# Cross-attention and a routed feed-forward on one core: GpSimd's instructions in another order, new first slots, kept rows as a full tile

## The reference, cut to what matters

```python
def xattn(input, feats):            # 16 heads of 16 features
    q = heads(input @ Wq + bq)
    k, v = heads(feats @ Wkv + bkv)
    scores = einsum('bhqd,bhkd->bhqk', q, k) / sqrt(D)
    attn = softmax(scores, axis=2)  # over the queries, not the keys
    return merge(einsum('bhqk,bhkd->bhqd', attn, v)) @ Wo + bo

def ffn(x):                         # 96 of 128 tokens of a batch
    scores = einsum('bld,d->bl', x, w_router)
    _, top_idx = top_k(scores, 96)
    processed = gelu(x[top_idx] @ w_block)       # tanh form
    return x.at[top_idx].set(processed)

x = x + xattn(layernorm(x), ctx_1024)
x = x + ffn(layernorm(x))
```

## Time and profile before

| what | value |
|---|---|
| time, median of 3 runs | 902.03 us (901.85 to 904.2) |
| the profiled execution's own time | 903.28 us |
| span, first to last instruction | 901.5 us |
| busy, share of the span: PE / PEld / DVE / ACT / POOL | 96% / 84% / 95% / 97% / 88% |
| granted TensorE clock, mean | 0.992 of full speed |
| DMA, share of 16 engines | 26% in queue 1, under 1% in the others |

### The profile page before, as it was taken

One profiled execution on the slowest core, in us unless ns is written; L12 is line 12 of the kernel. 1 busy time (PEld: TensorE's weight loads), 2 busy tenths in 40 slices (PEclk: granted clock), 3 DMA queues, 4 the chain that ended last, 5 costly groups with the idle time before them and its releaser, 6 DMA issues. The chain is left out here.

```text
span 901.5 us, 31626 instructions
## 1 busy us (share of the span) xinstructions
PE 868.3 (96%) x10562; PEld 755.4 (84%) x10562; DVE 854.4 (95%) x2068; ACT 872.5 (97%) x4632; POOL 795.0 (88%) x1487
## 2 busy tenths in 40 slices
PE   7899999999999999999999999999999999999972
PEld 6688888888888888888888888888888888888852
DVE  6889999999999999999999999999999999999987
ACT  5899999999999999999999999999999999999984
POOL 4568889999999999999999999999999999998865
PEclk9999999999999999999999999999999999999996
DMA  6221223233233223223223233223222222312102
GB/s 202 61 68 51 65 67 93 59 87 93 59 88 96 59 86 95 59 87 94 69 78 92 60 89 91 76 71 91 79 73 88 82 70 86 96 43 55 49 25 93
DMA packets 70978, 70.48 MB, mean 78 GB/s; under 512 B 12064, under 2 KB 62752, under 8 KB 70816
## 3 DMA queue, kind: packets, MB, share of 16 engines
q1 hardware_dynamic: 69456, 67.68, 26.2%
q10 hardware_dynamic: 1360, 0.79, 0.3%
HBM read 35.13 MB, written 16.78 MB: 58 GB/s over the span
## 5 line engine op out<-in xcount | busy, mean ns | idle before, releaser
L593 ACT ACTIVATE e_sb<-ps_s,neg_max 128x128 f32<-128x128 f32 x2048 | 770.0, 607 | 3.6 <-DVE neg_max L751 3.3
L593 ACT ACTIVATION_READ_ACCUMULATOR e_sb<-ps_s,neg_max 128x1 f32 x2048 | 704.0, 431 | 0.0
L751 DVE TENSOR_REDUCE neg_max<-ps_s 128x4 f32<-128x512 f32 x512 | 331.8, 668 | 25.8 <-PE ps_s L349 24.4
L349 PE MATMUL ps_s<-q_eo,k_sb 32*128 32x256 f32 x2048 | 146.6, 400 | 2.3 <-DVE recip L804 1.4
L414 PE MATMUL ps_a<-e_sb,v_pad 128*32 128x128 f32 x4096 | 138.4, 276 | 2.1 <-POOL v_pad L1085 0.9
L310 PE MATMUL ps_a<-w_o_sb,o_sb 128*128 128x256 f32 x512 | 133.2, 383 | 3.2 <-DVE v_sb L858 3.0
L414 PEld LDWEIGHTS ps_a<-e_sb,v_pad 128*32 128x32 f32 x4096 | 104.1, 109 | 23.7 <-issue 21.3
L349 PEld LDWEIGHTS ps_s<-q_eo,k_sb 32*128 32x128 f32 x2048 | 94.0, 184 | 30.8 <-issue 26.0
L1085 POOL TENSOR_TENSOR v_pad<-v_sb,recip 128x256 f32<-128x256 f32 x128 | 79.7, 623 | 31.8 <-DVE recip L811 29.8
L1074 POOL TENSOR_TENSOR x_sb<-x_sb,bo_sb 128x256 f32<-128x256 f32 x128 | 106.2, 831 | 0.2
L303 PE MATMUL ps_t<-w_z_hi,xt_hi 128*128 128x258 f32 x256 | 96.4, 376 | 2.2 <-DVE z_sb L870 2.2
(11 more groups left out here) (109 smaller groups left out, 2465.5 us busy)
## 6 DMA issues: line engine op xcount, KB each, us to landing
x_sb<-in_x SPq DMA_DIRECT2D x64, 256.0 KB, 2.9
c_sb<-in_ctx SPq DMA_DIRECT2D x64, 256.0 KB, 3.1
out<-z_sb SPq DMA_DIRECT2D x64, 256.0 KB, 2.4
q_eo<-q_raw SPq DMA_DIRECT2D x504, 32.0 KB, 2.0
z_sb<-in_L_xattn_Wkv ACTq DMA_DIRECT2D x2, 256.0 KB, 7.4
z_sb<-in_L_xattn_Wq ACTq DMA_DIRECT2D x1, 256.0 KB, 4.2
w_z_sb<-in_L_ffn_w_block SPq DMA_DIRECT2D x1, 256.0 KB, 7.7
w_o_sb<-in_L_xattn_Wo SPq DMA_DIRECT2D x1, 256.0 KB, 7.0
```

What stands on the lines that cost most here:

```text
L349: mm = nc.tensor.matmul(ps_s[:, bank(b, j), c, :, :], k_sb[rows, r2, c, h * T:(h + 1) * T], q_eo[rows, r2, :, c, h, :], start=True, stop=True)
L593: last = nc.scalar.activation(e_sb[:, b % 4, j, c, par, :], ps_s[:, bank(b, j), c, par, :], ACT.Exp, bias=neg_max[:, b % 4, h:h + 1], accu ...
L751: nc.vector.tensor_reduce(neg_max[:, b % 4, :].rearrange("p (c j q) -> p j c q", c=C, j=J)[:, j, :, :], ps_s[:, bank(b, j), :, :, :], AX.X ...
```

## The change

Four things change, and none of the arithmetic.

1. GpSimd's loop is reordered so that instructions with scalars and with two tensors alternate; `rstd1_of_pair` and `rstd2_of_pair` are split into a variance and a root, the values stand between them, input and bias directly behind the unprocessed row, and `gelu_square` always has its wait.
2. `gelu_product` works on batch s-8 in place of s-7, with the last one behind the loop.
3. The first slots of TensorE, ScalarE and VectorE have another order.
4. `keep_row` has 128 rows in place of 8, cleared once by a memset; its transpose is a full 128x128 one, of which VectorE reads the first 8 columns.

```diff
--- before.py
+++ after.py
@@ -98,7 +98,7 @@
         recip = sb("recip", [P, 4, H])
         cand = sb("cand", [GROUP, T])
         top8 = sb("top8", [GROUP, 8])
-        keep_row = sb("keep_row", [GROUP, T])
+        keep_row = sb("keep_row", [P, T])
         half_keep = sb("half_keep", [P, 2, GROUP])
         drop_rstd = sb("drop_rstd", [P, 2, GROUP])
         alpha = sb("alpha", [P, 2, GROUP])
@@ -125,7 +125,7 @@
         ps_xt = ps_q[:, 0:E]
         ps_z = ps_t[:, 0:ZW]
         ps_fifth = ps_s[:, J, :, :, :].rearrange("p c q t -> p (c q t)")
-        ps_cand, ps_keep, ps_mean = ps_fifth[0:GROUP, 0:T], ps_fifth[:, T:T + GROUP], ps_a[:, 0:ZW]
+        ps_cand, ps_keep, ps_mean = ps_fifth[0:GROUP, 0:T], ps_fifth[:, T:2 * T], ps_a[:, 0:ZW]
 
         def bank(b, j):
             return J if j == 0 and b % 2 == 1 else j
@@ -499,7 +499,7 @@
                 if b % GROUP == 0 and has(b):
                     pe.wait_ge(keep_row_ready, upto(b + 7))
                     pe.wait_ge(exp_ready[0], upto(b + 15))
-                    nc.tensor.transpose(ps_keep, keep_row[:, :], ident[0:GROUP, 0:GROUP]).then_inc(keep_mm, 8)
+                    nc.tensor.transpose(ps_keep, keep_row[:, :], ident[:, :]).then_inc(keep_mm, 8)
 
             transpose_inputs(0)
             transpose_inputs(1)
@@ -512,9 +512,9 @@
             queries_or_keys(2, 0)
             transpose_inputs(4)
             queries_or_keys(2, 1)
+            scores(1)
             mean_of_block_weights()
             transpose_inputs(5)
-            scores(1)
             values(0)
             transpose_inputs(6)
             queries_or_keys(4, 0)
@@ -666,8 +666,8 @@
             inputs_high(4)
             exps(0, 1)
             exps(0, 0)
+            exps(1, 3)
             inputs_high(5)
-            exps(1, 3)
             exps(1, 2)
             inputs_high(6)
             exps(1, 1)
@@ -898,13 +898,13 @@
                     dve.wait_ge(top_dropped, b + 8)
                     if has(b - 1):
                         dve.wait_ge(keep_mm, b)
-                    nc.vector.tensor_scalar(keep_row[:, ::-1], cand[:, :], LOWEST, None, ALU.is_gt).then_inc(keep_row_ready, 8)
+                    nc.vector.tensor_scalar(keep_row[0:GROUP, ::-1], cand[:, :], LOWEST, None, ALU.is_gt).then_inc(keep_row_ready, 8)
                 elif step == 10:
                     dve.wait_ge(keep_mm, b + 8)
                     dve.wait_ge(rstd2_ready, b + 8)
                     g, r = (b // GROUP) % 2, b % R
-                    nc.vector.scalar_tensor_tensor(drop_rstd[:, g, :], ps_keep, -1.0, rstd2[:, r:r + GROUP], ALU.add, ALU.mult)
-                    nc.vector.tensor_scalar(half_keep[:, g, :], ps_keep, 0.5, None, ALU.mult).then_inc(keep_col_ready, 8)
+                    nc.vector.scalar_tensor_tensor(drop_rstd[:, g, :], ps_keep[:, 0:GROUP], -1.0, rstd2[:, r:r + GROUP], ALU.add, ALU.mult)
+                    nc.vector.tensor_scalar(half_keep[:, g, :], ps_keep[:, 0:GROUP], 0.5, None, ALU.mult).then_inc(keep_col_ready, 8)
 
             def final(b, settled=False):
 
@@ -938,24 +938,24 @@
             inputs_low(3)
             for j in (3, 2, 1, 0):
                 maxima(0, j)
+            queries(2)
             weights_low("v")
-            queries(2)
             inputs_low(4)
+            inverse_sums_23(0)
+            keys(2)
             stats1_of_pair(6)
-            keys(2)
-            centre_block_weights()
-            inverse_sums_23(0)
             maxima(1, 3)
             maxima(1, 2)
+            centre_block_weights()
+            inverse_sums_01(0)
+            maxima(1, 1)
             inputs_low(5)
-            inverse_sums_01(0)
             values_and_bias(0)
-            maxima(1, 1)
             maxima(1, 0)
             inputs_low(6)
+            inverse_sums_23(1)
             stats1_of_pair(8)
             queries(4)
-            inverse_sums_23(1)
 
             for s in range(2, B):
                 sure = 20 <= s < B - 1
@@ -1037,20 +1037,26 @@
         @block.gpsimd
         def _(pool):
             nc.gpsimd.memset(ident[:, :], 0.0).then_inc(mask_step, 1)
+            nc.gpsimd.memset(keep_row[:, :], 0.0).then_inc(mask_step, 1)
             nc.gpsimd.memset(minus_half[:, :], -0.5).then_inc(mask_step, 1)
             nc.gpsimd.memset(w_z_sb[:, :, E + 1:E + 2], 0.0).then_inc(mask_step, 1)
             nc.gpsimd.memset(minus_mean[:, :], -1.0 / E).then_inc(mask_step, 1)
-            pool.wait_ge(mask_step, 4)
+            pool.wait_ge(mask_step, 5)
             nc.gpsimd.affine_select(out=ident[:, :], in_=ident[:, :], compare_op=ALU.not_equal, fill=1.0, base=0,
                                     pattern=[[-1, P]], channel_multiplier=1).then_inc(const_ready, 1)
             nc.gpsimd.memset(q_eo[:, 1, :, :, :, :], 0.0).then_inc(q_eo_zero, 1)
 
-            def rstd1_of_pair(b):
+            def variance1_of_pair(b):
 
                 if b % 2 == 0 and has(b):
                     r = slice(b % R, b % R + 2)
                     pool.wait_ge(st1_ready, upto(b + 1))
                     nc.gpsimd.tensor_scalar(ve1[:, r], m2_1[:, r], 1.0 / E, EPS, ALU.mult, ALU.add).then_inc(ve1_ready, 2)
+
+            def root1_of_pair(b):
+
+                if b % 2 == 0 and has(b):
+                    r = slice(b % R, b % R + 2)
                     nc.gpsimd.tensor_scalar(neg_m1[:, r], mean1[:, r], -1.0, None, ALU.mult)
                     pool.wait_ge(ve1_ready, upto(b + 1))
                     nc.gpsimd.tensor_tensor(rstd1[:, r], ve1[:, r], minus_half[:, :], ALU.pow).then_inc(rstd1_ready, 2)
@@ -1088,12 +1094,22 @@
                                             .to_broadcast([P, H // 2, 2, D]),
                                             ALU.mult).then_inc(v_pad_ready, 1)
 
-            def rstd2_of_pair(b):
+            def rstd1_of_pair(b):
+
+                variance1_of_pair(b)
+                root1_of_pair(b)
+
+            def variance2_of_pair(b):
 
                 if b % 2 == 0 and has(b):
                     r = slice(b % R, b % R + 2)
                     pool.wait_ge(st2_ready, upto(b + 1))
                     nc.gpsimd.tensor_scalar(ve2[:, r], m2_2[:, r], 1.0 / E, EPS, ALU.mult, ALU.add).then_inc(ve2_ready, 2)
+
+            def root2_of_pair(b):
+
+                if b % 2 == 0 and has(b):
+                    r = slice(b % R, b % R + 2)
                     pool.wait_ge(ve2_ready, upto(b + 1))
                     nc.gpsimd.tensor_tensor(rstd2[:, r], ve2[:, r], minus_half[:, :], ALU.pow).then_inc(rstd2_ready, 2)
 
@@ -1194,19 +1210,23 @@
             for s in range(4, B):
                 sure = 20 <= s < B - 1
                 normalise(s + 7, sure)
-                rstd1_of_pair(s + 9)
-                rstd2_of_pair(s - 4)
-                gelu_square(s - 5, sure)
+                gelu_square(s - 5)
+                variance1_of_pair(s + 9)
+                variance2_of_pair(s - 4)
                 values_over_sums(s - 1, sure)
+                root1_of_pair(s + 9)
+                root2_of_pair(s - 4)
                 scale_and_shift(s - 16)
                 unprocessed(s - 16, sure)
+                input_and_bias(s + 4)
                 gelu_factor(s - 5)
+                gelu_product(s - 8)
                 gelu_sum(s - 7)
-                input_and_bias(s + 4)
                 gelu_cubic(s - 5)
-                gelu_product(s - 7)
-
-            rstd2_of_pair(B - 4)
+
+            gelu_product(B - 8)
+            variance2_of_pair(B - 4)
+            root2_of_pair(B - 4)
             gelu_factor(B - 5)
             scale_and_shift(B - 16)
             values_over_sums(B - 1)
```

## The result

The changed kernel took **915.12 us** (median; 914.87 to 916.16) beside 901.94 us (901.66 to 904.2) for the kernel before: a ratio of 1.0145, 95% interval [1.0133, 1.0157]. It is slower by 13 us, where 899.3 us was forecast. Two executions among those of the experiments (970.84 and 1210.61 us, at granted clocks of 0.85 and 0.65 in the mean) are left out of all medians and ratios. The profiled execution took 915.23 us (span 913.4).

| stretch | before | after | difference |
|---|---|---|---|
| to score matmul 16 | 124.20 | 122.47 | -1.73 |
| 13 groups of 8 steps, each | 53.63 | 54.72 | +1.09, in all +14.17 |
| score matmul 120 to 127 | 45.84 | 45.00 | -0.84 |
| score matmul 127 to the end | 34.3 | 34.6 | +0.3 |

The account below looks back on a forecast made before the run. It took ScalarE's casts to bound the main loop, 53.52 us a group, TensorE's group being 0.12 us above. Terms -1.2 (loop), -1.3 (start) and -0.2 (rest) sum to -2.7 us: 902.03 to 899.3 us, range 897.6 to 902.4.

Parts of the forecast that it names:

- What the order moves: Main loop: GpSimd's new order makes its input-and-bias sum delay VectorE's final sum, 0.24 us a group against 0.10 before.
- rival 2: Main loop: GpSimd wins the port in steps without second norm and with kept rows; 54.06 us a group, 906.0 us; chance 0.10.
- The alternation: GpSimd's loop: each broken-up pair gives 0.12 us, some 0.4 us a step, costed at nothing because GpSimd waits for reciprocals anyway.
- Kept rows: TensorE's full-tile transpose, one step in eight: 0.13 us in place of 0.35; with collisions, main loop gains 1.2 us.
- ScalarE's floor: Main loop: ScalarE's casts, 6.69 us apart, allow no group of eight steps under 53.52 us.
- First slots: Kernel start: reordered lists start score matmuls 1 and 2 near 22.0 and 29.85 us, gaining 1.3 us.
- The rest: Memset, later gelu product and last steps: net -0.2 us, mostly from fewer final-sum stalls at the end.

Follow-up runs that it names:

- The three kernels with late sums in some steps: Changed kernel, sum of input and bias moved behind the gelu sum only in steps 0; 5, 6, 7; or 1 to 7: 912.59, 904.48, 902.02 us.
- the late sum: Changed kernel with only GpSimd's sum of input and bias moved back behind the gelu sum, in all steps: 899.21 us.

## Why the prediction was wrong

**The step that failed** is the one under "What the order moves": 0.24 us a group for the collisions of L1074 (now L1080) with the final sum. Measured against the changed kernel's steps it is 1.46 us: TensorE's own 53.04 + 0.11 + 0.11 = 53.26 us stand against 54.72. By the starts of the transposes and of L394 behind the scores (means, beside the kernel with the old order) it is made of:

| place | forecast | measured |
|---|---|---|
| the four odd steps | 2 x 0.12 | 0.08, 0.08, 0.13, 0.27 |
| steps 2, 4 and 6 | 0 | 0, -0.02, 0.09 |
| step 0, transposes | 0 | 0.50 |
| step 0, VectorE's lag at the keys | 0 | 0.32 |

A step's delay is the one of the transposes that follow its final sum. These add up to 1.45 (the expectations of two runs have 0.36 for the last one; the traces give 0.32). Three assumptions were in it.

- **Who loses.** I let half of the odd steps go free, because in the kernel before GpSimd once started 0.13 us ahead and still waited. In the changed kernel GpSimd was first in every step of the main loop and held VectorE up in all but step 4 of each eight and one step 7, with leads of 0.07 to 0.47 us by the records (in step 4 it was at least 0.63 us ahead and nearly done). The 2.32 us from reciprocals to final sum were also read off a step with router work; in steps 1 and 3 they are 2.21 to 2.22, so L1080 had a lead of only 0.13 us there, and it won all the same.
- **Step 0.** I treated it as an even step and left its two small instructions (beta, alpha) to rival 2, at 0.30. There they put the row to 2.36 us behind the reciprocals, L1080 runs to 3.06, and the final sum takes 0.94 us, 0.52 too many. Nearly all of that, 0.50, is on the path.
- **The free time.** I took 0.18 us off each step's delay as if each step had it anew. In steps 5, 6, 7 and 0 VectorE has hardly any idle time, 0 to 0.06 us in the group below (fourth number of each row, beside the step's length); what the final sum loses in one is still missing in the next, until TensorE waits for the keys. The three kernels with late sums in some steps show this: taking the collisions out of steps 5 to 7 gives back 0.86 us a group, though these steps' own delays at the transposes are 0.13, 0.09 and 0.27; with them goes the 0.32 us at the keys in step 0.

```profile
485.15:491.78 6.63, 6.63 (x87) 5.81 (x83) 6.63 (x17) 6.63 (x38) 5.92 (x13) 1.00 0.16 50
491.78:498.51 6.73, 6.69 (x86) 5.80 (x82) 6.73 (x18) 6.73 (x38) 6.03 (x12) 1.00 0.50 145
498.51:505.23 6.72, 6.70 (x86) 5.81 (x82) 6.72 (x18) 6.72 (x38) 6.10 (x12) 1.00 0.06 16
505.23:512.63 7.40, 6.99 (x87) 5.92 (x83) 7.34 (x20) 7.27 (x39) 6.12 (x14) 1.00 0.41 116
```

**What was right.** The mechanism, rival 2: GpSimd wins, VectorE comes second, the transposes are late. It had 0.10 of the chances and 54.06 us a group, 0.66 too few, as it too priced each step by itself. Its point, that a lead of 0.15 us decides, holds in the kernel before and fails in the changed one, where leads of 0.07 and 0.13 us won (last section). The second-norm steps came as worked out, final sums of 0.42 to 0.68 us for 0.62, and nearly all of it hidden.

**The alternation**, costed at nothing: right. GpSimd's waits for reciprocals grew from 29.8 to 72.3 us, and the fastest kernels with and without the alternation are 898.22 and 898.8 us.

**Kept rows**: 0.13 us forecast, 0.11 measured; the step 6.74 us without collisions, "about 6.8" forecast. A group without collisions is 53.43 us, where 53.55 was taken and 53.52 held to be ScalarE's floor; that is less than 53.52, so this was no floor. ScalarE is busy for 641.15 of 641.18 us there and TensorE for 640.94; which of them binds isn't separated.

**First slots**: 22.0 and 29.85 forecast, 21.85 and 29.59 measured; 1.3 us forecast, 1.73 in the changed kernel's trace and 1.4 alone.

**The rest**, -0.2 us: -0.84 in the last steps, where the final sums are 0.42 to 0.71 us in steps 121 to 127 for up to 0.99 before, and +0.3 behind score matmul 127.

So the other terms come near their sizes: the kernel with the old order and both other parts takes 898.8 us, where 899.3 was forecast for the whole change. It has neither the failed term nor what the new order gives at the end, so the two times are not quite of the same sum.

## What to carry to other kernels

An engine that is 98% busy, as VectorE was here, has little slack, and what it has need not lie in the steps that lose: follow its lag over the whole period of the schedule and not step by step. Before a list is tightened, ask what each instruction will then meet on the engine that it can block, or that can block it; a tighter list can fix a bad phase in nearly every step, where the loose one met it in about one of sixteen. And put the instruction that must not wait at a place where the other engine ends one, not where it starts one.

## What was not expected of the hardware

The starts in the records don't tell who waits, within about 0.15 us. In the kernel before GpSimd started 0.13 us ahead and waited; in the changed kernel it started 0.13 us ahead and won (464.10 and 464.23); with the late sum its factor started 0.03 us behind the final sum (457.47 and 457.44) and still won. In the two last cases the row for which the final sum waits had ended 0.1 us or less before the final sum's start (464.13, 457.39), in the first one over 1 us before (484.20 + 0.56); it may be that the wait makes VectorE ask later than its record says, which no run here isolates. In the twelve traces, over score matmuls 16 to 120, the sum of input and bias started up to 0.15 us ahead of the final sum 221 times. In 156 of them the row had ended 0.1 us or less before the final sum (leads of 0.06 to 0.13 us), and GpSimd won them all; in the other 65 it had ended over 0.9 us before (leads of 0.03 to 0.15 us), and GpSimd waited in all. With leads of 0.2 us and more it never waited. The two sorts also differ in what stood just ahead on GpSimd, the row in the first and the gelu sum in the second, so which of the two counts stays open. The kernel before has only the second sort, so its trace could not show the first.

The Trainium skill, "SBUF — State Buffer", section "Who interferes with whom", has it that issue order and not the kind of instruction decides who blocks. The prediction held the trace of before against that; the runs behind it agree with the rule better than I then said, if issue isn't read from the records' starts: blocked by a two-tensor or by a scalar instruction, VectorE's sum ends 0.27 to 0.29 us behind it.
